# A scan moved ahead of the token-shift subtraction on VectorE, in a gated linear recurrence with a channel-mix block

## The reference

```python
g = x @ Wg + bg;  v = x @ Wv + bv;  d = x @ Wd + bd
h[t] = a[t] * h[t-1] + sigmoid(g[t]) * tanh(v[t])      # a = 0.001 + 0.998 * sigmoid(d), per channel
x1 = layernorm(x + h)

xp = x1 shifted by one step in time (0 ahead of the first)
xr = mu_r * x1 + (1 - mu_r) * xp;  xk = mu_k * x1 + (1 - mu_k) * xp
out = layernorm(x1 + sigmoid(xr @ W_r.T) * (relu(xk @ W_k.T) ** 2 @ W_v.T))
```

## Time and profile before

| what | us |
|---|---|
| median of 2 runs (1210.62 to 1213.29) | 1211.96 |
| the profiled execution | 1215.06 |
| its span, first to last instruction, slowest core (core 4) | 1213.4 |
| spans of the eight cores | 1196.5 to 1213.4 |
| TensorE busy | 888.0 |
| VectorE busy | 662.3 |
| ScalarE busy | 551.0 |
| GpSimd busy | 526.5 |

### The profile page before, as it was taken

How to read it: one execution, slowest core, us unless ns; L and a number is a source line. 1 busy time by engine, 2 the same in 40 slices (tenths; PEclk the granted TensorE clock), 3 DMA queues, 4 the chain that set the end, 5 groups by cost and what they waited for, 6 DMA issues and landing times.

```text
span 1213.4 us, 21179 instructions; the slowest of 8 cores (1196.5 to 1213.4 us)
## 1 busy us (share of the span) xinstructions
PE 888.0 (73%) x6528; PEld 675.3 (56%) x6528; DVE 662.3 (55%) x1039; ACT 551.0 (45%) x1182; POOL 526.5 (43%) x784
## 2 busy tenths in 40 slices
PE   2471469687878878797878888787969688874554
PEld 1351348475757566584757565665748475743342
DVE  1434153655658483846555574838465555747454
ACT  2120235445463645455454635454555546452331
POOL 4668634344445344443344453444434433532201
PEclk9675779798889889898989888898979898996877
DMA  6669211121110112121211111121212120110102
GB/s 189 205 183 298 83 49 36 35 71 35 43 64 21 51 35 70 35 71 36 70 36 46 59 36 36 36 70 36 70 36 71 35 69 3 36 36 1 35 1 70
DMA packets 46811, 75.83 MB, mean 62 GB/s; under 512 B 3184, under 2 KB 36976, under 8 KB 46704
## 3 DMA queue, kind: packets, MB, share of 16 engines
q0 software_dynamic: 11712, 39.85, 10.2%
q1 hardware_dynamic: 18096, 17.85, 4.9%
q10 hardware_dynamic: 16896, 16.78, 4.1%
HBM read 57.69 MB, written 16.78 MB: 61 GB/s over the span
## 4 chain that ended last, share of the span: by engine, by line
PE 43%; ACT 16%; DVE 15%; issue 13%; POOL 6%; DMA 5%; DVEq 0%; ACTq 0%; POOLq 0%; SPq 0%
PE po L634 8%; PE psb L581 7%; PE pg L569 5%; PE pv L569 5%; PE pkr L614 5%; PE pkk L614 5%; PE pd L569 4%; ACT rk L402 4%; ACT kab L405 4%; DVE z L518 3%; POOL xs L239 2%; PE psb L588 2%; DVE row_t L500 2%; DVE xrk L533 2%; DVE row_mq L496 2%
## 5 line engine op out<-in xcount | busy, mean ns | idle before, releaser
L569 PE MATMUL pg<-xbf,wbwg 128*128 128x256 bf16 x1024 | 161.5, 311 | 164.1 <-ACT sg L355 107.9
L290 POOL TENSOR_TENSOR z<-z,xnew 128x256 f32<-128x256 f32 x120 | 128.6, 1072 | 243.6 <-DVE carry L463 225.9
L569 PEld LDWEIGHTS pg<-xbf,wbwg 128*128 128x128 bf16 x1024 | 106.2, 109 | 218.0 <-issue 196.5
L239 POOL TENSOR_TENSOR xs<-sg,tv 128x256 f32<-128x256 f32 x128 | 118.7, 928 | 167.3 <-ACT sd L361 163.8
L569 PE MATMUL pv<-xbf,wbwv 128*128 128x256 bf16 x1024 | 160.6, 309 | 0.0
L355 ACT ACTIVATE sg<-pg,bpk_s 128x256 f32<-128x256 f32 x128 | 60.5, 473 | 220.1 <-POOL aa L241 140.8
L549 DVE TENSOR_TENSOR z<-rbuf,po 128x256 f32<-128x256 f32 x128 | 54.0, 422 | 179.4 <-PE po L634 179.4
L569 PE MATMUL pd<-xbf,wbwd 128*128 128x256 bf16 x1024 | 147.6, 292 | 0.0
L634 PE MATMUL po<-kab,wbwvf 128*128 128x256 bf16 x1024 | 114.4, 272 | 21.8 <-ACT kab L405 21.8
L569 PEld LDWEIGHTS pv<-xbf,wbwv 128*128 128x128 bf16 x1024 | 114.0, 111 | 25.6
L458 DVE TENSOR_TENSOR_SCAN z<-aa,carry,xs 128x256 f32<-128x256 f32 x128 | 117.9, 921 | 13.0 <-DVE carry L463 6.6
(11 more groups left out here) (137 smaller groups left out, 1546.6 us busy)
## 6 DMA issues: line engine op xcount, KB each, us to landing
xnew<-xT SPq DMA_DIRECT2D x32, 512.0 KB, 4.7
yT<-y ACTq DMA_DIRECT2D x32, 512.0 KB, 4.1
stage<-xT POOLq DMA_DIRECT2D x28, 512.0 KB, 4.8
stage<-wg POOLq DMA_DIRECT2D x6, 256.0 KB, 5.3
stage<-wv POOLq DMA_DIRECT2D x6, 256.0 KB, 5.4
xrk<-wd POOLq DMA_DIRECT2D x6, 256.0 KB, 5.5
xrk<-wg POOLq DMA_DIRECT2D x6, 256.0 KB, 3.7
kab<-wv POOLq DMA_DIRECT2D x6, 256.0 KB, 5.3
```

The source lines that it names most:

```text
L239: INC(g.tensor_tensor(out=blk(xs, ke), in0=half(sg, ke % 2), in1=half(tv, ke % 2), op=ALU.mult), "pool", s_attnv, 1)
L290: INC(g.tensor_tensor(out=blk(Z(i + 1), ke), in0=blk(Z(i + 1), ke), in1=blk(xnew, ke), op=ALU.add), "pool", s_z, 1)
L569: ins = t.matmul(out=bank[:, 0:N], lhsT=wtile(w, ke, kd), rhs=xbf_blk(ti, kd), start=(kd == 0), stop=(kd == NB - 1))
```

## The change

The call for scan 2 is put ahead of the subtraction into rbuf and its fence; before it stood behind them. Nothing else differs. The subtraction is L529 in the changed kernel, and L527 in the one before.

```diff
                 W(v, "vec", s_pass, i + 1)
                 if i == 0:
                     W(v, "vec", s_misc, 16)
+                if i + 1 <= NT - 1:
+                    scan_one(i + 1, 2)
                 idt = v.tensor_tensor(out=rbuf_blks, in0=y1v_full, in1=xpv_full,
                                       op=ALU.subtract)
                 vfence(v, idt)
-                if i + 1 <= NT - 1:
-                    scan_one(i + 1, 2)
                 for ke in range(NB):
```

## The result

The changed kernel takes 1221.9 us in the median against 1210.4 us of the kernel before on the same chip: ratio 1.0093, 95% interval 1.0077 to 1.0108. A second series on another chip gave 1.0103 (1.0076 to 1.0130). Some executions of both kernels are slow, with a lower granted clock on one die (1242 to 1288 us for the changed one here), and the ratios of this document leave them out. So the change makes the kernel slower by about 1%, 11 us, where 6.7 us were forecast.

What follows compares the result with a forecast made beforehand. A ring of waits among engines bounds it; the fourth scan's start sets each tile. 13 x 0.37 = 4.8 us, tile 14's 0.5 and the clock's 1.4 make 6.7, on a median of 1211.96: 1218.7 us, range 1209.5 to 1227.

Steps and rivals of the forecast that it cites:

- Step 1: VectorE's waits: with no other engine about, the swap is worth nothing; xr starts at 703.73 instead of 703.70.
- Step 2: GpSimd's addition of block 1 beats the moved third scan, which takes 1.27 us instead of 0.75.
- Step 3: VectorE's subtraction waits for GpSimd's xs of block 0, so xr starts 0.65 us late.
- Step 4: xr meets less GpSimd work, 4.33 us instead of 4.61, leaving the fourth scan 0.37 us late per tile.
- Tile 14: No trio left, TensorE waits for xr itself; no xs delays the subtraction, so 0.5 us late.
- Step 5: Longer idle time before TensorE's sixth trio brings one more fall of the clock, 1.4 us; bounds none and 18.7.
- One sign of being right: TensorE's wait for ScalarE's sg was to go up by 4 to 6 us over all.
- rival D: Longer idle time before the sixth trio drops the clock in most tiles, 1.44 us each; 1236.0 us if all 13; chance 0.12.
- Rival B: Collisions with GpSimd do not fall on VectorE, so not slower: 1208.7 us; chance 0.12.
- Rival C: The fourth scan comes later, but something else covers it before the sixth trio: about 1212 us; chance 0.14.

Runs made afterwards that it cites:

- e1: Kernel before, GpSimd's additions of blocks 1 and 2 and, from tile 2 on, xs and aa of blocks 0 and 1 on 8 of 256 columns; median core 1035.4 us from first L520.
- e2: Changed kernel, GpSimd's additions of blocks 1 and 2 and, from tile 2 on, xs and aa of blocks 0 and 1 on 8 of 256 columns; median core 1048.0 us.
- e7: Changed kernel, but GpSimd's addition of block 1 waits for the third scan's carry instead of the second's; 1227.3 us, one time only.
- e8: Kernel before with the fourth scan moved ahead of the eight xr, behind the third; ratio 0.9825.
- e9: Kernel before with the fourth scan ahead of xr, and GpSimd's xs and aa of block 0 ahead of its addition of block 1; ratio 0.9474.
- e4: Kernel before with two more instructions of the form of xr, into a scratch tile, ahead of the fourth scan; ratio 1.0234.
- e3: Kernel before with one more instruction of the form of xr, into a scratch tile, ahead of the fourth scan; ratio 1.0066.
- e5: Changed kernel with eight unused 128x256 matmuls on TensorE ahead of the sixth trio; ratio 1.0056 against the kernel before.

## Why the prediction was right, and where it was short

The direction and the range were right (1221.9 in 1209.5 to 1227), and so was the mechanism of the collisions, step by step. The effect was forecast as 6.7 us and measured as 11; that the forecast time of 1218.7 is only 3.2 us off is in part luck, since it was built on a median of two runs that lay 1.6 us above the later one.

- Step 1, that the order of waits is worth nothing by itself: shown by e1 and e2, within 0.03 us.
- Step 2, scan meets addition: the scan was to end at 4.63 us behind L520, and ended at 4.62. Its length is 1.19 us and not 1.27, since it starts 0.08 us later than the addition and not beside it.
- Step 3, the subtraction meets xs: to end at 7.29 behind L520, ended at 7.30; xr at 7.40 as forecast.
- Step 4, 4.33 us for xr: as forecast. Fourth scan 0.36 us late where 0.37 was said. The mean over all tiles is 0.31, because in tiles 6 and 7 the kernel before had stalls of its own that the new order hides; 4.0 us instead of 4.8.
- Tile 14: 0.2 us instead of 0.5. xr starts at 7.18 and not 7.24, and takes 3.53 us and not 3.71: the prediction let the addition of block 2 meet xr as before, but in the new order it starts beside the subtraction, at 1104.83, waits it out, and ends 0.48 us into xr, where it ended 1.05 us into xr before.
- **Step 5 is the term that was mis-sized.** It gave the clock one more fall per core, 1.4 us, and said that it took one between none and thirteen. The traces show 3.4 more per core (62 in 208 tiles against 8), 4.8 us. The bound was right and the pick was not. It was read from one core, with one fall in 13 tiles. The same trace holds all eight: 12 of its 104 tiles idled 1.9 us or more and 5 of them fell, and another 41 idled 1.4 to 1.9 us, which 0.5 us more carries across. At the same rate that makes 22 falls instead of 5, 2.1 more per core, or 3 us instead of 1.4 (an estimate from these counts).
- One sign of being right did not come: TensorE's wait for sg was to grow by 4 to 6 us and grew by 2.4 in the mean over the cores. The sign named for rival D did: L614 over 2.7 us behind the sixth trio in several tiles.

Rival B (collisions that cost VectorE nothing) falls by the scan's 1.19 us. Rival C (no effect on the r products) falls: in the changed kernel no first r product of tiles 1 to 13 comes before 19.95 us behind L520, where ten of these tiles had 19.59 in the kernel before (tiles 6 and 7, with stalls of their own, had 19.98 and 20.08 and are no later now unless the clock falls). Rival D was right in kind, at 4 tiles of 13, which is where the prediction had it begin to outweigh the collisions; the late fourth scan (4.0 us) and the clock (4.8 us) each make about half of what is explained. The Trainium skill's "SBUF — State Buffer", section "Who interferes with whom", which the prediction weighed, says that issue order decides who waits. The runs bear that out: the scan waits for the addition in the changed kernel (1.19 us), and in e7 the addition for the subtraction (2.63 us). Its letter, a block for the whole instruction, would have put the scan's end at 4.83; it was 4.62.

## What to carry to other kernels

An independent instruction that looks like good filling for a fence can cost more than the fence. Ask what the neighbour engine does at that moment: here the waits behind a long instruction were a place in which GpSimd's queued work cost VectorE nothing, and filling them moved that work onto the path. Where TensorE idles for nearly long enough to lose its clock, price a short delay by counting, over all cores, how many tiles stand just below the idle time at which falls begin. And follow the chain to the instruction whose start sets the end: moving the fourth scan ahead of xr (e8) gave a ratio of 0.9825, and with it moving xs ahead of an addition that nobody waits for (e9) one of 0.9474, where the swap of two neighbours made without that question lost 1%.

## What the runs showed of the hardware that I had not expected

- The same work given to TensorE earlier made the kernel slower: e2 against e1, 12.6 us, with the sixth trio starting at the same time and 5.0 instead of 2.6 us of idle time in front of it.
- 0.39 us more of delay in e4 than in e3 took the tiles with late r products from 19 to 84 of 104, and 0.9 us of products that nobody uses took them from 32 to none (e5).
- An instruction of GpSimd on 8 columns was held up by VectorE's subtraction like one on 256 columns: beside the subtraction of e2 shown above, the xs of block 1, on 8 columns, took 2.15 us, and the addition on as many columns, ahead of the subtraction, 0.20 (at 691.79). GpSimd in tile 8 of core 0 of e2:

```profile
692.99 2.15 POOL L240 TENSOR_TENSOR xs<-sg,tv 128x8 f32<-128x8 f32 x1
```
